# Dealing the row products of a graph-attention layer among three engines, and GpSimd's place for them

## The reference, cut to what matters

```
h = (x @ W.T).reshape(n, 8, 32)
h_src, h_dst = h[src], h[dst]
alpha = sum(h_src * a_src) + sum(h_dst * a_dst)              # per edge and head
enc = relu(edge_attr @ edge_W.T + edge_b).reshape(-1, 8, 32)
alpha = leaky(alpha + sum(enc * h_dst))
ex = exp(alpha - amax[dst]);  denom = segment_sum(ex, dst)
out = segment_sum(h_src * ex / denom[dst], dst) + bias
x = layernorm(x + out)
```

## Time and profile before

| | |
|---|---|
| median of 3 runs | 2146.94 us (2145.23 to 2147.84) |
| profiled execution | 2150.75 us, span 2148.9 us |
| mean granted TensorE clock | 0.844 |
| busy over the span | PE 1676.9 us (78%), DVE 1659.5 (77%), POOL 1552.5 (72%), ACT 1071.4 (50%) |
| gathers | 1320, 1284.2 us on POOL (L1225) |
| row products on POOL | 200, 129.0 us (L1237) |
| row products on ACT | 1840 activations, 511.3 us over all layers (L1414) |
| row products on DVE | 480, 216.0 us over all layers (L815) |

### The profile page before, as it was taken

One profiled execution on the slowest core, in us unless ns is written; L12 is line 12 of the kernel. 1 busy time (PEld: TensorE's weight loads), 2 busy tenths in 40 slices (PEclk: granted clock), 3 DMA queues, 4 the chain that ended last, 5 costly groups with the idle time before them and its releaser, 6 DMA issues. The chain is left out here.

```text
span 2148.9 us, 42137 instructions
## 1 busy us (share of the span) xinstructions
PE 1676.9 (78%) x9240; PEld 1039.6 (48%) x9240; DVE 1659.5 (77%) x4633; ACT 1071.4 (50%) x3670; POOL 1552.5 (72%) x1714
## 2 busy tenths in 40 slices
PE   7387888888885667778777776578999999899884
PEld 5244544544453434445444444345555555555551
DVE  5578877777779546666666667868999999999988
ACT  3134443443342435445455553546666666666655
POOL 3767777777777377777777776567778877778763
PEclk9578777877876868887888887879999999999985
DMA  6754444455640244444444641243444444444421
GB/s 195 178 144 134 140 139 137 138 140 155 185 124 29 89 127 136 135 135 134 134 130 135 198 121 37 91 124 106 130 135 132 127 125 129 132 130 134 133 67 60
DMA packets 131322, 274.32 MB, mean 128 GB/s; under 512 B 40389, under 2 KB 65968, under 8 KB 131061
## 3 DMA queue, kind: packets, MB, share of 16 engines
q0 software_dynamic: 64128, 181.33, 30.5%
q1 hardware_dynamic: 62259, 86.45, 13.4%
q10 hardware_dynamic: 4699, 3.86, 0.6%
HBM read 255.34 MB, written 17.20 MB: 127 GB/s over the span
## 5 line engine op out<-in xcount | busy, mean ns | idle before, releaser
L1225 POOL DMA_INDIRECT rows<-table,index_all x1320 | 1284.2, 973 | 481.1 <-issue 344.0
L1658 PE MATMUL bank<-rows,onehot 128*128 128x264 f32 (+1 forms) x2640 | 984.7, 483 | 178.1 <-ACT rows L1414 91.1
L826 DVE TENSOR_TENSOR sums<-sums,bank 128x264 f32 (+1 forms) x1320 | 552.7, 419 | 202.5 <-PE bank L1658 106.1
L1658 PEld LDWEIGHTS bank<-rows,onehot 128*128 128x128 f32 x2640 | 498.4, 224 | 386.7 <-ACT rows L1414 153.1
L1414 ACT ACTIVATE rows<-rows,wgt 128x33 f32<-128x33 f32 (+2 forms) x1840 | 511.3, 358 | 0.1
L1366 ACT CAST onehot<-bank 128x768 f32<-128x768 bf16 x240 | 177.7, 742 | 197.6 <-PE bank L1581 193.9
L1422 ACT ACTIVATE prod<-bank 128x512 f32<-128x512 f32 x240 | 134.8, 562 | 205.7 <-PE bank L1670 185.4
L815 DVE TENSOR_TENSOR rows<-rows,wgt 128x260 f32<-128x260 f32 (+2 forms) x480 | 216.0, 450 | 0.7 <-ACT wgt L1407 0.6
L1677 PE MATMUL bank<-late,onehotT 128*128 x1320 | 193.9, 283 | 0.7 <-DVE prod L835 0.7
L1373 ACT COPY scoreT<-bank 44x256 f32<-44x256 f32 (+2 forms) x120 | 39.5, 329 | 274.4 <-PE bank L1611 224.0
L835 DVE TENSOR_TENSOR prod<-prod,bank 128x512 f32<-128x512 f32 x240 | 151.8, 632 | 11.5 <-PE bank L1677 6.9
(11 more groups left out here) (200 smaller groups left out, 1787.6 us busy)
## 6 DMA issues: line engine op xcount, KB each, us to landing
locb<-loc_d SPq DMA_DIRECT2D x120, 352.0 KB, 3.8
rows<-table,index_all POOLq DMA_INDIRECT x1320
flags<-flags_d SPq DMA_DIRECT2D x520, 27.5 KB
table<-rows SPq DMA_DIRECT2D x25, 136.0 KB, 1.9
table<-rows SPq DMA_DIRECT2D x25, 134.0 KB, 3.0
late<-table SPq DMA_DIRECT2D x1, 3300.0 KB
table<-rows SPq DMA_DIRECT2D x25, 129.5 KB, 2.0
late<-table SPq DMA_DIRECT2D x1, 3212.5 KB, 14.8
```

The source lines that it names most:

```text
L826: done(v.tensor_tensor(a, a, sum_bank(l, t, s)[:, 0:VV], ALU.add), "add")
L1225: g.indirect_dma_start(out=rows[:, t.u, s, 0:ROW[l]], out_offset=None, in_=table[l], in_offset=bass.IndirectOffsetOnAxis(ap=index_all[:, t ...
L1658: done(m.matmul(sum_bank(l, t, s)[:, 0:VV], onehot[:, t.u, s, :], rows[:, t.u, s, 0:VV], start=True, stop=True), "agg")
```

## The change

In layer 2, VectorE keeps the products of slots 0 and 1 and gives up that of slot 3. ScalarE has slots 3, 5, 7, 9 in place of 2, 5, 8. GpSimd has 2, 4, 6, 8, 10 in place of 4, 6, 7, 9, 10. GpSimd's `period` of batch t now gathers batch t + 3's first two groups, multiplies batch t + 1's slots, and then gathers the last group; batch 0's products go ahead of the loop. Layers 0 and 1 have no products on GpSimd, and their gathers keep their order.

```
-OWNER = ("VAVVAVAVVVV", "VAAAAAAAAAA", "VVAVPAPPAPP")
+OWNER = ("VAVVAVAVVVV", "VAAAAAAAAAA", "VVPAPAPAPAP")
...
-                def gather(t, l=l):
+                def gather(t, groups=GATHERS, l=l):
                     old = not isinstance(t.j, int) or t.k >= RING
-                    for lo, hi in GATHERS:
+                    for lo, hi in groups:
...
-                def period(t, left, l=l):
+                def muls(t, l=l):
                     for s in OWN[l]["P"]:
                         mul(t, s)
+
+                def period(t, left, l=l):
                     if left > 3:
-                        gather(t.after(3))
+                        gather(t.after(3), GATHERS[:-1])
+                    if left > 1:
+                        muls(t.after(1))
+                    if left > 3:
+                        gather(t.after(3), GATHERS[-1:])
                     if left == 2:
                         finished(0)
+                muls(Batch(0, 0))
                 batches(pool, period)
```

## The result

The changed kernel takes 2258.76 us (median of 4, 2255.6 to 2261.03), the kernel before 2147.39 beside it: a ratio of 1.0513, interval 1.0498 to 1.0527, or 111 us slower. The forecast was 2214, range 2172 to 2272. The direction and the range held; the sum gave 67 us where 111 were lost, and the result lies outside the 2195 to 2230 of the prediction's own case, in the part of the range that its two dearest rivals had opened.

The account below looks back on a forecast made before the run. A 17.00 us batch loop was taken as bound by TensorE up to add 7, then VectorE. Product 3 at 0, relu +0.90 and collisions +1.06 made 18.96; 34 x 1.96 = 67 us gave 2214 us against the median, range 2172 to 2272.

Parts of the forecast that it names:

- the prediction's own case: Relu delay plus collisions over 34 batches, chance 0.50: 2203 to 2223 us, 2195 to 2230 with start and drain.
- its two dearest rivals: Granted clock falls once per batch (chance 0.14, 2268 us); full blocking of VectorE by GpSimd's products (chance 0.07, 2265 us).
- the loop of 17.00: Steady last-layer batch from add 0 to add 0, 17.00 us: TensorE sets it up to add 7, VectorE afterwards.
- the prediction's own signs: Checks in the trace: GpSimd product starts 18.9 us apart; wrong if the clock leaves 1.00 between 1510 and 2040.
- Product 3 off VectorE, worth 0: Product 3 lies between add 0 and add 4, where add 4 waits for TensorE anyway: 0 of its 0.63 us.
- Face 6's relu, +0.90: ScalarE's product 7 delays exponential and face 6's relu, and through the register load add 7: +0.90 us per batch.
- Collisions, +1.06, range 0.31 to 1.33: L739, L745, product 1 and L753 on VectorE lengthen beside GpSimd's moved products: +1.06 us per batch.
- the 0.2 for each of the three small operations: Assumed lengthening of L739, L745 and L753 beside GpSimd's products: 0.2 us each, between 0 and 0.29.
- the cap of 0.29 from L782: Upper value per small operation, from VectorE's L782 taking 0.64 us beside GpSimd's products against 0.35.
- The rival with full blocking: Each of four VectorE operations pays a whole GpSimd product, 2.56 us instead of 1.06: 2265 us, chance 0.07.
- The clock, left at 1.00 in the sum: Granted clock stays full in the main sum; its fall, 1.6 us per batch, was a rival: 2268 us, chance 0.14.
- Start and drain, 3 x 1.96 = 6 us in the sum: 1.96 us counted for 34 batches, 3 to 36; batches 0 to 2 and 37 to 39 taken as 0, plus or minus 3.

Follow-up runs that it names:

- product 3 alone moved: Kernel before, with product 3 from VectorE to GpSimd and product 9 to ScalarE, old GpSimd order: 2181.66 us, ratio 1.0164.
- order-only kernel: The changed kernel's GpSimd queue order with the old dealing of products to engines: 2235.53 us, ratio 1.0398.
- the kernel with the moved load: Changed kernel with VectorE's block register load at step 4 instead of 7, ahead of face 6: 2216.67 us, ratio 1.0302; on a slower chip 1.0048.
- the dealing alone: Kernel before with the new dealing (GpSimd 2 4 6 8 10, ScalarE 3 5 7 9) and the old GpSimd order: 2216.82 us, ratio 1.0300.
- product 7 alone: Kernel before, with product 7 moved to ScalarE and product 8 to GpSimd: 2177.16 us, ratio 1.0135.
- the cut products: Changed kernel with each GpSimd product cut to the first column of each head, the rest unmultiplied: 2175.15 us in one execution.
- the changed kernel's waits filled: Changed kernel with sixteen extra matmuls before each of TensorE's two waits per batch: 2241.37 us, ratio 1.0402; on a slower chip 1.0244.

## Why the prediction came out as it did

In the profiled executions the loss is 2253.8 - 2148.9 = 104.9 us: 31 x 2.84 = 88 in the steady stretch (17.12 to 19.96), 5 in the batches ahead of it, 12 behind. From the loop of 17.00, the period is 17.00 + 0.78 (relu) + 1.52 (collisions) = 19.3, which is what GpSimd's intervals without a fall measure (six of the 31, 19.27 to 19.46); the falls bring 19.96. Direction and mechanism were right, and the size came out low: 2258.76 lies above the prediction's own case (2195 to 2230), and the range holds it because it had been opened for the rivals at 2265 and 2268. Two of the prediction's own signs speak against it: the products start 19.96 apart and not 18.9, and the clock left 1.00.

**Product 3 off VectorE, worth 0: right.** Add 4 waits 0.48 after the change and 0.49 with product 3 alone moved; the gain turned into that wait. The order-only kernel, which keeps product 3, has 18.6 between its products without a fall, 17.00 and its collisions.

**Face 6's relu, +0.90: right, 0.78 measured.** The chain copy, exponential, relu, load, add 7 is there link by link; the load follows the relu by 1.64 where 1.73 were taken.

**Collisions, +1.06, range 0.31 to 1.33: the place right, the size too small; 1.52.** What failed is the 0.2 for each of the three small operations and the cap of 0.29 from L782: L739 costs 0.39, L745 0.32, L753 0.35, and only product 1 was right (0.46). Scans do not leave the port free. This is 0.46 x 31 = 14 us of the difference. The small ones do not pay less for being small: the price of each is the rest of the GpSimd product that it meets. The prediction set the blocking aside because 0.86 is less than 0.40 and a whole product of 0.64. But that VectorE product began at 2106.63, 0.24 behind GpSimd's at 2106.39, and what was left of GpSimd's is all that it had to wait for. The rival with full blocking had the mechanism, then, and priced it at four whole products, 2.56, where four rests of products were paid, 1.52. The Trainium skill (SBUF — State Buffer, "Who interferes with whom") has the later instruction fully blocked until the other ends; the trace agrees, with the 122 ends behind a product's end. It does not cover L745 in the kernel with the moved load, which had begun first. The page's rule which instructions meet agrees too: `add`, with one input in a PSUM bank, stays at 0.41 to 0.43. Gathers lengthen none of these rows. Both sides pay: GpSimd's five products take 3.45, and 3.00 where nothing meets them.

**The clock, left at 1.00 in the sum: the other step that failed.** It was priced as a rival with 0.14, on top of the sum, once a batch. It came: of 618.7 us some 95 at half speed, a mean of 0.92. Where the batch without a fall takes 19.3, the mean takes 19.96: 0.64 x 31 = 20 us, some 5 of them in two batches of 22.5 and 21.5 with longer falls. That is less than the 1.6 a batch that the earlier trace rows gave, as the one that was followed, at 1638.7, lengthened four matmuls by 0.7 and little else that the loop waits for. The argument against it, 31 batches at 1.00, was one about a loop in which TensorE waits little. The period does not order the kernels: at 18.6 the clock is 0.97 with the dealing alone and 0.91 with the order alone. TensorE's longest waits between matmuls, from the traces of the 31 batches, order them better. With one wait of over 1 us a batch the clock is 1.00 (the kernel before; 1.1 us), 0.99 (product 7 alone, the cut products; 1.3), 0.97 (the dealing alone; 1.3, and more short ones) and 0.94 (the moved load; 1.6). With two, together 3.1 to 3.3 us, it is 0.91 (the order alone) and 0.92 (the changed kernel), and with the changed kernel's waits filled 0.98. Of these only the filling was made as a test of TensorE's waits; the order of the others is an observation.

**Start and drain, 3 x 1.96 = 6 us in the sum: 17 measured.** Not taken apart; the batch at 2135 has the same collisions, and the mean clock of what follows the 31 batches is 0.67, against 0.68 before.

So 67 predicted against 105: relu -4, collisions +14, clock +20, start and drain +11, and -4 because the mean batch before was 17.12 and not 17.00: 104.

**The parts do not stand alone.** Dealing alone costs 62.6, order alone 88.9, both together 102.6 to 111: the order cures the dealing's own wait (slot 2, 0.84 a batch) and puts the collisions in its place.

## What to carry to other kernels

Before an engine is relieved, find the half of the loop on which it sets the time: a product taken from the other half only makes its next wait longer. Where GpSimd's arithmetic is moved, look which VectorE instructions with both inputs in SBUF it will lie beside, scans and small ones too, and price each at what is left of the GpSimd instruction that it meets: up to 0.6 us beside products of 0.60 to 0.65, 0.3 to 0.5 for the ones in a row here, not less for a shorter instruction. And when a sum gives TensorE new idle time in every period, add the clock's fall to that sum rather than pricing it as an alternative.

## What the runs showed that was not expected

- The half-speed pieces are 3.4 us long, a few 6.8 or 10.2. What one costs depends on where it falls: some 0.6 to 0.7 us in the usual batch of 19.9 to 20.0.
- More TensorE work made a kernel faster: 32 added matmuls a batch, 2256.76 to 2241.37 us.
- A collision costs what is left of the GpSimd product, not a share of the VectorE instruction's own length: L739 takes 0.28, 0.44, 0.64 or 0.73 when it comes 0.55, 0.37, 0.16 or 0.07 behind the product's start (the last in the kernel with the order alone). Even L772, eight elements in one partition, takes 0.61 beside GpSimd's products in the kernel with the dealing alone (1629.77, in a product from 1629.73 to 1630.36), and 0.16 in the changed kernel.
- A row's releaser can be wrong by an engine: slot 2 was put down to an add that had ended 0.97 us earlier.
